# The output takes the place of one table of routed rows: scatter-adds into the result, an add from memory to memory at the end, early weights and eight result buffers

## The reference

```
logits = flat @ Wr + router_bias
topk_scores, topk_idx = top_k(softmax(logits), 4)      # normalised to sum 1
xb = zeros(E, CAP, D).at[eid, pos].set(flat[tok], mode='drop')
h  = silu(einsum('ecd,edh->ech', xb, Wg)) * einsum('ecd,edh->ech', xb, Wu)
yb = einsum('ech,ehd->ecd', h, Wd)
y  = yb[eid, min(pos, CAP - 1)] * (w * valid)[:, None]
out = zeros(N, D).at[tok].add(y)
out = out + sum over s of (silu(flat @ Sg[s]) * (flat @ Su[s])) @ Sd[s]
x   = x + tanh(g) * out
```

## Time and profile before

| | |
|---|---|
| median of 3 runs | 1182.45 us (1178.94 to 1184.02) |
| profiled execution | 1178.42 us |
| its span in the trace | 1176.7 us |
| busy: PE, PEld, DVE, ACT, POOL | 89%, 63%, 57%, 41%, 47% |
| DMA moved | 206.54 MB, mean 176 GB/s |
| PE busy by 1/40 of the span, in tenths | 3999999999879999997798799999998999999920 |

### The profile page before, as it was taken

The page is one execution under the profiler, slowest core; times in us unless marked ns, Lnnn a source line. Parts: engine busy times, 40 slices in busy tenths (PEclk is TensorE's granted clock), DMA queues, the critical chain, the costliest instruction groups (busy, mean ns, idle before and its releaser), DMA issues. The chain is left out here.

```text
span 1176.7 us, 18454 instructions
## 1 busy us (share of the span) xinstructions
PE 1045.8 (89%) x5324; PEld 735.5 (63%) x5324; DVE 675.2 (57%) x1558; ACT 480.4 (41%) x835; POOL 552.2 (47%) x517
## 2 busy tenths in 40 slices
PE   3999999999879999997798799999998999999920
PEld 2555555555437777774498377586687777787710
DVE  4677777776458888884677256265312333343426
ACT  2465565564338888886322121222212222222200
POOL 4344544644426666666415557446151344333530
PEclk9999999999989999998899899999998999999965
DMA  9976555773534333333610131130029999999639
GB/s 294 345 235 204 169 181 203 252 252 99 197 134 168 103 105 107 107 108 105 217 34 27 75 102 37 41 122 13 27 83 328 362 342 301 279 323 344 146 89 361
DMA packets 133243, 206.54 MB, mean 176 GB/s; under 512 B 36743, under 2 KB 44935, under 8 KB 133178
## 3 DMA queue, kind: packets, MB, share of 16 engines
q1 hardware_dynamic: 113274, 172.72, 43.4%
q0 software_dynamic: 19616, 32.50, 10.1%
q10 hardware_dynamic: 288, 0.52, 0.1%
HBM read 137.56 MB, written 87.03 MB: 191 GB/s over the span
## 5 line engine op out<-in xcount | busy, mean ns | idle before, releaser
L1922 POOL DMA_INDIRECT sums<-summary,m_token x64 | 99.2, 1550 | 161.2 <-DVE summary L1996 86.2
L906 POOL TENSOR_TENSOR m_down_lo<-wo,m_down_hi 128x512 fp32r<-128x512 f32 x80 | 133.0, 1682 | 79.7 <-ACT m_down_hi L1001 79.7
L514 PE MATMUL bank<-win,vT 128*128 128x512 f32 x256 | 124.2, 598 | 0.0
L604 ACT ACTIVATE win<-bank 128x512 f32<-128x512 f32 x128 | 69.5, 595 | 109.4 <-PE bank L506 109.2
L674 DVE TENSOR_REDUCE negmax<-bank 128x1 bf16<-128x512 f32 x128 | 87.0, 679 | 43.3 <-PE bank L521 43.0
L1015 DVE TENSOR_TENSOR m_up_lo<-w,m_up_hi 128x1024 fp32r<-128x1024 f32 x80 | 98.3, 1230 | 12.0 <-ACT m_up_hi L973 10.9
L521 PE MATMUL bank<-k_hi,q_parts 128*128 128x512 f32 x128 | 76.8, 600 | 17.0 <-DVE negmax L674 13.4
L1945 PE MATMUL bank<-y,m_w 128*128 128x128 f32 x736 | 89.7, 275 | 0.0
L1235 POOL DMA_INDIRECT tab<-stage_up,slot x64 | 66.3, 1036 | 49.2 <-DVE slot L1570 31.0
L1945 PEld LDWEIGHTS bank<-y,m_w 128*128 128x128 f32 x736 | 86.4, 193 | 0.5 <-issue 0.5
L2100 PE MATMUL bank<-w_sd,stage_gate 128*128 128x512 f32 x192 | 84.9, 598 | 0.3 <-DVE stage_gate L2090 0.3
(11 more groups left out here) (282 smaller groups left out, 2383.8 us busy)
## 6 DMA issues: line engine op xcount, KB each, us to landing
tab<-zeros SPq DMA_DIRECT2D x16, 1056.0 KB
m_w<-in_L_ffn_Wg SPq DMA_DIRECT2D x46, 256.0 KB, 5.3
m_w<-in_L_ffn_Wu SPq DMA_DIRECT2D x46, 256.0 KB, 5.9
m_w<-in_L_ffn_Wd SPq DMA_DIRECT2D x46, 256.0 KB, 6.2
m_x<-tab SPq DMA_DIRECT2D x40, 256.0 KB, 2.6
ytab<-m_y SPq DMA_DIRECT2D x40, 256.0 KB, 2.0
stage_up<-tab SPq DMA_DIRECT2D x32, 264.0 KB, 7.4
m_x<-tab SPq DMA_DIRECT2D x32, 264.0 KB, 5.7
```

The source lines that it names most:

```text
L514: nc.tensor.matmul(pO[s * 2 + h][:], vT[:, s, sb_, h:h + 2, :].rearrange("p a c -> p (a c)"), probs[:, sb_ % 2, h, :], start=(sb_ == 0), s ...
L604: nc.scalar.activation(probs[:, b % 2, h, :], pS[h][:], ACT.Exp, scale=1.0 / HEAD).then_inc(p_ready, 1)
L906: nc.gpsimd.tensor_tensor(dn_lo[:, m, :], row(wo0, e * MB + m), dn_hi[:, m, :], ALU.subtract).then_inc(dn_lo_ready, 1)
L1922: nc.gpsimd.indirect_dma_start(T["sums1"][e % SUMS], bass.IndirectOffsetOnAxis(token[:, e % META:e % META + 1], 0), y[:, e % RING, :], Non ...
```

## The change

- The table `sums1_1` is gone. Experts with an odd number scatter-add straight into `out`; so only one table is zeroed. Before that SP stores x to `out`, in four pieces of 1 MB as the groups of `middle` are done (`store`), the last group without its shared part.
- At the end the one table left is added to `out`. For groups 0 to 2 POOL issues three DMAs of 1 MB from memory to memory that add to their destination (256 pieces of 4 KB each). For the last group SP loads the table's 1 MB into `rest`, DVE adds the shared part that was kept aside in `x_sb`, and POOL adds `rest` to `out` with a fourth DMA from the on-chip memory. `finish` and its block are gone.
- Result buffers: 8 (`RING`), in a tile of their own; the semaphores `added` count by table, not by buffer.
- Early weights: the split weights are laid out by shared expert, so that the half that belongs to the first shared expert comes free after 4 of the last group's 8 slices. Experts 4 to 8 are loaded then, ahead of the routed rows; only expert 3 is left behind the last slice.

```
-W_EARLY = 6
+W_EARLY = 9
...
-        sums1 = [nc.dram_tensor(f"sums1_{n}", (B * SEQ, D), F32, kind="Internal").ap() for n in range(SUMS)]
+        sums1 = nc.dram_tensor("sums1", (B * SEQ, D), F32, kind="Internal").ap()
+        out_rows = out.rearrange("b t d -> (b t) d")
+        out_begun = ctx.enter_context(nc.semaphore("out_begun"))
...
-                T["w_hi"], T["w_lo"] = (sb(n, [P, 2, NSH, DB * HSH], F32R, splits, "right") for n in ("w_hi", "w_lo"))
+                T["w_hi"], T["w_lo"] = (sb(n, [P, NSH, 2, DB * HSH], F32R, splits, "right") for n in ("w_hi", "w_lo"))
...
-            finish(nc, A, T, out)
...
+            def store(g, ready, value):
+
+                tiles = slice(g * TPB, g * TPB + TPB)
+                sp.wait_ge(ready, value)
+                sp.dma_start(T["out_rows"].rearrange("(t p) d -> p t d", p=P)[:, tiles, :],
+                             x_sb[:, tiles, :]).then_inc(T["out_begun"], 16)
+
+            for g in range(2):
+                store(g, shared.y_read, g * TPB + TPB)
             sp.wait_ge(x2_ready, TILES - TPB)
             for e in range(2):
                 load_expert(sp, A, T, e, e)
+            store(B - 1, x3_ready, TILES)
             sp.wait_ge(lg_full, TILES)
             sp.wait_ge(fT_kept, TILES)
             load_expert(sp, A, T, 2, 2)
-
+            store(B - 2, shared.y_read, TILES - TPB)
+
+            sp.wait_ge(shared.up_full, chunk(B - 1, HSH // P - 1) + 1)
+            for e in range(4, W_EARLY):
+                load_expert(sp, A, T, e, e)
             sp.wait_ge(scattered, 16 * TILES * TOP1)
             for e in range(X_EARLY):
                 load_rows(sp, T, e)
             sp.wait_ge(shared.up_full, chunk(B - 1, SharedExperts.CHUNKS - 1) + 1)
-            for e in range(3, W_EARLY):
-                load_expert(sp, A, T, e, e)
+            load_expert(sp, A, T, 3, 3)
...
-        RING = 4
+        RING = 8
...
-        y = T["summary"]
-        added = [sem(f"m1_added_{n}") for n in range(RING)]
+        y = sb("m1_y", [P, RING, D])
+        added = [sem(f"m1_added_{n}") for n in range(SUMS)]
...
+            sp.wait_ge(added[0], 16 * E1 // SUMS)
+            sp.dma_start(rest[:], T["sums1"].rearrange("(t p) d -> p t d", p=P)[:, TILES - TPB:, :]).then_inc(rest_loaded, 16)
...
-                    T["sums1"][e % SUMS], bass.IndirectOffsetOnAxis(token[:, e % META:e % META + 1], 0), y[:, e % RING, :], None,
-                    bounds_check=B * SEQ - 1, oob_is_err=False, compute_op=ALU.add).then_inc(added[e % RING], 16)
-            for s in range(RING):
-                pool.wait_ge(added[s], 16 * E1 // RING)
+                    tables[e % SUMS], bass.IndirectOffsetOnAxis(token[:, e % META:e % META + 1], 0), y[:, e % RING, :], None,
+                    bounds_check=B * SEQ - 1, oob_is_err=False, compute_op=ALU.add).then_inc(added[e % SUMS], 16)
+            for s in range(SUMS):
+                pool.wait_ge(added[s], 16 * E1 // SUMS)
+            whole, part = (t.rearrange("(n p r) d -> n p (r d)", n=PARTS, p=P) for t in (T["out_rows"], T["sums1"]))
+            for n in range(PARTS - 1):
+                nc.gpsimd.dma_start(whole[n], part[n], max_dma_last_dim=2 * 4 * D, accum_op=ALU.add).then_inc(stored, 16)
+            pool.wait_ge(rest_ready, 1)
+            nc.gpsimd.dma_start(T["out_rows"].rearrange("(t p) d -> p t d", p=P)[:, TILES - TPB:, :], rest[:],
+                                accum_op=ALU.add).then_inc(stored, 16)
+            pool.wait_ge(stored, 16 * PARTS)
...
                     if i > RING:
-                        dve.wait_ge(added[(i - 1) % RING], 16 * ((i - 1) // RING))
+                        dve.wait_ge(added[(i - 1 - RING) % SUMS], 16 * ((i - 1 - RING) // SUMS + 1))
...
+            dve.wait_ge(rest_loaded, 16)
+            nc.vector.tensor_tensor(rest[:], rest[:], x_sb[:, TILES - TPB:, :], ALU.add).then_inc(rest_ready, 1)
```

More of the change, by code:

```diff
@@ L305, in _ @@
             t1 = T["tab1"].rearrange("(n r p) d -> n p r d", p=P, n=ZERO_CHUNKS)
-            sums = [t.rearrange("(n r p) d -> n p r d", p=P, n=E0) for t in T["sums1"]]
+            sums = T["sums1"].rearrange("(n r p) d -> n p r d", p=P, n=E0)
             w01_v = w01[:].rearrange("p (e b) m -> p e b m", e=E0)
@@ L325, in behind @@
                         [P, E1 * CAP1 // (ZERO_CHUNKS * P), XW])).then_inc(s_zero1, 16)
[L326 to L329, removed]
+                chunk = sums[u] if isinstance(u, int) else sums[bass.ds(u, 1)].rearrange("o p r d -> p (o r) d")
+                sp.dma_start(chunk, zeros[:, 0:D].unsqueeze(1).broadcast_to(
+                    [P, B * SEQ // (E0 * P), D])).then_inc(s_zero1, 16)
             behind(0)
@@ L1181, in split_weights @@
             eng.wait_ge(hi_ready, n + 1)
-            return ops.tensor_tensor(w_lo[:, w, s, :], stage[w][:, s, :], w_hi[:, w, s, :], ALU.subtract)
+            return ops.tensor_tensor(w_lo[:, NSH - 1 - s, w, :], stage[w][:, s, :], w_hi[:, s, w, :], ALU.subtract)
         def first_stat(a, n):
@@ L1417, in first_part @@
                 for w, s in which:
-                    nc.scalar.copy(w_hi[:, w, s, :], stage[w][:, s, :]).then_inc(hi_ready, 1)
+                    nc.scalar.copy(w_hi[:, s, w, :], stage[w][:, s, :]).then_inc(hi_ready, 1)
             def exp_weights(g):
@@ L1892, in experts @@
         BACK = 4
+        PARTS = 4
+        tables = T["sums1"], T["out_rows"]
+        rest = T["summary"]
+        rest_loaded, rest_ready, stored = sem("rest_loaded"), sem("rest_ready"), sem("out_stored")
         block = c.enter_context(nc.Block())
@@ L2000, in _ @@
                     dve.wait_ge(back_full, j + 1)
[L2001 to L2009, removed]
-        def sb(name, shape, dt=F32):
-            return c.enter_context(nc.sbuf_tensor(name, shape, dt))
-        def sem(name):
-            return c.enter_context(nc.semaphore(name))
-        x_sb = T["x_sb"]
-        RING = 4
-        part = sb("part", [P, RING, SUMS, D])
-        loaded = [sem(f"sums_loaded_{n}") for n in range(RING)]
-        combined, stored = sem("combined"), sem("out_stored")
-        out_v = out.rearrange("b (t p) d -> p (b t) d", p=P)
-        sums = [t.rearrange("(t p) d -> p t d", p=P) for t in T["sums1"]]
-        block = c.enter_context(nc.Block())
-        @block.sync
-        def _(sp):
-            for t in range(TILES + RING - 1):
-                if t < TILES:
-                    need(sp, combined, t - RING + 1)
-                    for n in range(SUMS):
-                        sp.dma_start(part[:, t % RING, n, :], sums[n][:, t, :]).then_inc(loaded[t % RING], 16)
-                if t >= RING - 1:
-                    k = t - RING + 1
-                    sp.wait_ge(combined, k + 1)
-                    sp.dma_start(out_v[:, k, :], x_sb[:, k, :]).then_inc(stored, 16)
-            sp.wait_ge(stored, 16 * TILES)
-        @block.vector
-        def _(dve):
-            for t in range(TILES):
-                dve.wait_ge(loaded[t % RING], 16 * SUMS * (t // RING + 1))
-                for n in range(SUMS):
-                    last = nc.vector.tensor_tensor(x_sb[:, t, :], part[:, t % RING, n, :], x_sb[:, t, :], ALU.add)
-                    if n < SUMS - 1:
-                        dve.drain()
-                last.then_inc(combined, 1)
@@ L2049 @@
+                    if j == 0:
+                        dve.wait_ge(T["out_begun"], 16 * B)
+                    nc.vector.tensor_scalar(x_sb[:, (B - 1) * TPB + j, :], pB[j % 2][:], T["gates"][:, 3:4], None,
+                                            ALU.mult).then_inc(back_read, 1)
+            dve.wait_ge(rest_loaded, 16)
+            nc.vector.tensor_tensor(rest[:], rest[:], x_sb[:, TILES - TPB:, :], ALU.add).then_inc(rest_ready, 1)
 class SharedExperts:
@@ L2078, in up @@
                     wc = slice(d * HSH + at, d * HSH + at + P)
-                    last = nc.tensor.matmul(out, w[:, k, s, wc], x[:, d, cols], start=(d == 0 and part == 0),
+                    last = nc.tensor.matmul(out, w[:, k, wc], x[:, d, cols], start=(d == 0 and part == 0),
                                             stop=(d == DB - 1 and part == 2))
```

14 lines of the change are left out of this document (8 added, 6 removed).

## The result

The changed kernel takes 1164.68 us (median of 4 runs, 1162.68 to 1168.85), beside 1182.03 us for the kernel before on the same chip (4 runs, 1178.94 to 1184.02): a ratio of 0.9863, 95% interval 0.9836 to 0.9891, or 16 us less with 13 to 19 in the interval. 1165 us was predicted. So the two spans differ by only 9.6 us.

A forecast was written before the change was run, and what follows sets the result against it. PE was taken to set `experts`, with some 50 us of transfer-filled tail behind it. The span's end, 1137.0 + 2.1 + 27.5 + 1.5 = 1168.1 less 7.2, is 1160.9 against 1176.7; predicted time 1165 us, range 1153 to 1179.

The forecast's parts named there:

- the front's gain: Up to the last scatter-add's issue: early weights and buffers save 2.8 + 2.4 + 2 = 7.2 us, range 3 to 9.
- Seam: Step into `experts`: six of nine loads leave SP's queue behind the last slice, so PE starts 2.8 us sooner.
- Clock: Start of `experts`: with 1.8 us idle in place of 4.6 PE's clock may hold, saving 2.4 us, else 0.
- Eight buffers: Late in `experts`: PE's two large waits go and results come earlier; bounds 0 and 3.9 us, 2 taken.
- Zeroes and stores at nothing: `attention` and `middle`: moved zeroes and stores are covered by dense PE and nearly free DMA engines; 0 to 12 us, 0 taken.
- Streaming of the adds: Tail: 4.19 MB of adding take 27.5 us, 19.2 for three large DMAs and 8.3 for the fourth.
- Around the adds: Tail: release 5.65 us after the last scatter-add's issue, 2.1 us to first data, 1.5 us from last data to landing.
- The rest hidden: Tail: the rest's load and DVE's addition are over by 1142, hidden since POOL needs them only after three DMAs.
- the slow add: Tail rival: each piece waits for source, then destination, 0.52 us per 2 KB; 66 us of data, time near 1203; chance 0.09.
- the one in between: Tail rival: streaming of 38 to 48 us and the rest as forecast, about no change; chance 0.10.
- the adds at copy speed: Tail rival: adds run like copies, 11.5 us of data, 16 less, about 1149 us; chance 0.15.
- The rival of no gain from weights and buffers: `experts`: 7.2 us are lost, as the start or clock doesn't improve and landings bind the scatter-adds; about 1172; chance 0.14.

The follow-up runs named there:

- u1_seam: Changed kernel with the old weights: experts 3 to 5 loaded behind the last slice, none ahead of the routed rows; 1172.41 us, ratio to before 0.9929.
- u2_ring4: Changed kernel with four result buffers in place of eight; 1165.66 us, ratio to before 0.9857.
- m2_8k: Changed kernel with pieces of 8 KB in place of 4 KB in the three memory-to-memory adding DMAs; 1165.79 us, ratio to before 0.987.
- u3_oldtail: Kernel before with only the early weights and eight buffers, keeping two tables and the old `finish`; 1178.29 us, ratio to before 0.9983.
- m5_single: Changed kernel with the fourth adding DMA as four indirect ones, each issued when all before it have landed; 1181.33 us in one run, before 1179.38.
- m4_indirect: Changed kernel with the fourth adding DMA as four indirect ones, rows in order, queued behind the large adds; 1165.41 us, ratio to before 0.987.
- u4_restlate: Changed kernel with the load of `rest` waiting for both tables' scatter-adds, not the first table's alone; 1167.02 us, ratio to before 0.9878.
- i1_tiles: Changed kernel adding the last group's shared part to table 0 inside `experts`, ending with four memory-to-memory adds in 8 KB pieces; 1171.42 us, ratio to before 0.9909.
- i2_spwait: Changed kernel with SP in place of POOL waiting for the four adding DMAs at the end; 1167.34 us, ratio to before 0.9884.

## Why the prediction was right, and where it was not

The total came out right (15.4 us in the stages, 16 by the times, 15.8 predicted), but with luck, as two errors cancelled: the front's gain was put 2.8 us too high and the tail's 2.4 too low.

- **Seam**: right. The gap is 2.85 us shorter (2.8 predicted), and u1_seam brings the long one back.
- **Clock**: right in the profiled execution, where seam and clock together give 5.0 us at the third expert's transposes (5.2 predicted). But it is no sure gain: with the same gap the clock fell in three kernels of eleven, and their stage ended no later. So of the 2.4 us nothing is to be seen at the stage's end. What makes the front's 4.4 us out of the seam's 2.85 no run isolates.
- **Eight buffers**: wrong, 2 us predicted, nothing measured. PE's late waits go, as I said, and that they aren't the stage's end I had said too; the 2 us rested on results coming earlier to POOL. u2_ring4 shows that PE's waits don't set that end: they return and the time doesn't change, while two thirds of POOL's waiting is for landings. The lower bound of that term was the right value, and the rival's "buffers bring nothing, as the scatter-add chain is bound by landings" holds.
- **Zeroes and stores at nothing**: no cost is to be seen. m2_8k arrives at the last slice when before did, u3_oldtail without stores is as long in `middle`, and the 16 us of the times (13 to 19) leave nothing beside the 15.4 of the two stages, give or take 3.
- **Streaming of the adds**: the mis-sized term. 27.5 us were predicted, 22 to 23 measured. The step that failed was to carry the scatter-add's 0.26 us a row over to a deep queue. The row was read rightly, but it belongs to a lone short DMA; m5_single reproduces it, and m4_indirect with the same form in a queue is at 0.18. By pieces: 768 x 0.35 / 16 = 16.9 us for the large adds (19.2 predicted) and 512 x 0.18 / 16 = 5.8 for the last (8.3). The rule of the Trainium skill that I set aside ("Collectives: The Full Stack", section "The bandwidth ceiling: the fold count and why AG ≠ RS ≠ AR": the add costs its second source read, so half the copy rate; it stands there for a reduction between cores) gave an estimated 23 us. Measured are 22 to 23 us, 174 to 190 GB/s beside 364 GB/s of copies, and m2_8k to m4_indirect agree at three sizes.
- **Around the adds**: three small terms were off. The release came 7.05 us after the last issue, not 5.65, because the rest's load ran beside that landing (5.30 in u4_restlate and 5.17 in i1_tiles without it). From issue to data were 1.4 us, not 2.1. From the last data to the end were 4.2 us, not 1.5: the sum had the landing and left out POOL's DRAIN of 3.2 us. Sum for the tail: 7.05 + 1.4 + 21.8 + 4.2 = 34.4, where I had 5.7 + 2.1 + 27.5 + 1.5 = 36.8.
- **The rest hidden**: right. DVE's addition ends at 1140.10, POOL asks at 1141.53.

Of the rivals, the slow add (66 us of data), the one in between (38 to 48) and the adds at copy speed (11.5) are all excluded by the slices of the tail. The rival of no gain from weights and buffers holds for the buffers, and for the clock in some kernels.

## What to carry to other kernels

Price a stream of adding DMAs by the byte, at about half the rate of copies (174 to 190 GB/s beside 364 here), and not by the row of a lone short DMA, whose packets look half as long again. A wait that disappears is worth something only if the chain that ends the stage runs through it: look at what the last instruction of the stage waits for, and put the other waits at zero. A clock that holds in one profile is no gain yet: look at other executions, and at whether the stage's end moves with it. Compare two profiles from an event that both share, since the way there can differ by 6.9 us between kernels that are alike up to it.

## What was not expected of the hardware

- An adding DMA of 128 rows of 2 KB takes 0.25 to 0.27 us a row and engine by itself and 0.18 with others queued around it. Which part of a lone DMA's packets is waiting no run shows.
- Behind the last landing of its DMAs POOL's DRAIN takes another 3.2 us in the changed kernel and 3.4 us behind a last DMA of 256 KB (m5_single), and it ends 2.8 us behind the landing even where it began 23 us ahead of it (i2_spwait). What it waits for is open. At the end of `middle` it takes 7.9 us, before and after.
- After gaps of 3.56 and 3.39 us at the same place the granted clock held in one execution and fell to the lower level in the other, for the same instructions. After 1.75 us at the start of `experts` it held in eight kernels and fell in three. What decides it no run shows.
